# An attention sink folded into TensorE's accumulation, and the last score tile reduced in one piece

## The reference

```python
q = einsum('bsd,pd->bsp', x, w_q) + b_q          # 129 wide
k = einsum('bsd,pd->bsp', x, w_k) + b_k
v = einsum('bsd,ed->bse', x, w_v) + b_v
k_full = concatenate([k_0, k]);  v_full = concatenate([v_0, v])
attn = softmax(einsum('bqp,bkp->bqk', q, k_full))
x = layernorm(x + (x + einsum('bqk,bkd->bqd', attn, v_full)))
lilora_weight = up_aux @ (lora_up @ (lora_down @ down_aux))
x = layernorm(x + x @ W.T + b + x @ lilora_weight.T)
```

## Time and profile before

| | |
|---|---|
| time, median of 2 runs | 457.05 us (456.87 to 457.23) |
| the profiled execution's own time | 455.76 us |
| its span, slowest core (7) | 454.1 us |
| spans of the eight cores | 442.2 to 454.1 us |
| mean granted TensorE clock | 0.927 to 0.965 |
| busy: TensorE / VectorE / ScalarE | 370.0 / 227.8 / 105.7 us |

### The profile page before, as it was taken

The page is one execution under the profiler, slowest core; times in us unless marked ns, Lnnn a source line. Parts: engine busy times, 40 slices in busy tenths (PEclk is TensorE's granted clock), DMA queues, the critical chain, the costliest instruction groups (busy, mean ns, idle before and its releaser), DMA issues.

```text
span 454.1 us, 5184 instructions; the slowest of 8 cores (442.2 to 454.1 us)
## 1 busy us (share of the span) xinstructions
PE 370.0 (81%) x1861; PEld 156.0 (34%) x1861; DVE 227.8 (50%) x375; ACT 105.7 (23%) x119; POOL 22.5 (5%) x46
## 2 busy tenths in 40 slices
PE   0745999999878678889999999999745888899991
PEld 0211333333423223334444444444312334333330
DVE  7000033333399910004766677666688525677673
ACT  0203100000000048952121211212142232423332
POOL 8400000000000000010000000000110000000000
PEclk9997999999899969999999999999957559999997
DMA  8999300000000020024212213121390001232322
GB/s 126 166 168 168 52 0 0 1 0 0 1 1 1 0 93 0 1 44 103 64 49 62 78 48 95 46 81 59 69 149 16 0 1 46 95 139 104 130 122 110
DMA packets 11097, 28.25 MB, mean 62 GB/s; under 512 B 1856, under 2 KB 3008, under 8 KB 11072
## 3 DMA queue, kind: packets, MB, share of 16 engines
q0 software_dynamic: 5712, 10.52, 15.0%
q1 hardware_dynamic: 5360, 17.41, 11.0%
HBM read 29.50 MB, written 8.39 MB: 83 GB/s over the span
## 4 chain that ended last, share of the span: by engine, by line
issue 25%; DVE 24%; PEld 13%; PEldq 9%; DVEq 9%; DMA 8%; ACT 7%; POOL 3%; ACTq 0%; SPq 0%; POOLq 0%
DMA Ke<-PTsink 8%; PEld pv L377 5%; DVE pq L636 4%; PEld pq L516 4%; ACT o1s L746 4%; DVE mcols L588 4%; DVE X1f L665 3%; DVE st L654 2%; DVE ys L649 2%; PEldq L525 2%; DVEq L653 2%; DVEq L656 2%; PEldq L441 2%; DVE modd L592 2%; DVE modd L593 1%
## 5 line engine op out<-in xcount | busy, mean ns | idle before, releaser
L461 PE MATMUL pq<-Vh,AR 128*128 128x512 bf16 x256 | 97.2, 380 | 0.0
L460 PE MATMUL pq<-Vh,AR 128*128 128x512 bf16 x256 | 96.4, 377 | 0.0
L516 PE MATMUL pq<-Vh,AR 128*128 128x512 bf16 x256 | 62.3, 387 | 6.2 <-issue 5.0
L581 DVE TENSOR_TENSOR Vh<-pv,X1f 128x1024 bf16<-128x1024 f32 x16 | 19.6, 1226 | 84.9 <-PEq L381 84.9
L377 PE MATMUL pv<-AR 128*128 128x512 bf16 x256 | 57.8, 379 | 4.3 <-issue 3.5
L459 PE MATMUL pv<-Vh,AR 128*128 128x1 bf16 x256 | 42.0, 164 | 6.5 <-issue 4.8
L636 DVE SCALAR_TENSOR_TENSOR pq<-Vs,packf,pq 128x1024 f32<-128x1024 bf16 x16 | 20.6, 1289 | 48.0 <-PEq L462 45.5
L459 PEld LDWEIGHTS pv<-Vh,AR 128*128 128x128 bf16 x256 | 25.0, 98 | 42.7 <-issue 13.9
L516 PEld LDWEIGHTS pq<-Vh,AR 128*128 128x128 bf16 x256 | 24.2, 99 | 40.9 <-issue 15.8
L377 PEld LDWEIGHTS pv<-AR 128*128 128x128 bf16 x256 | 23.9, 97 | 38.2 <-issue 11.7
L460 PEld LDWEIGHTS pq<-Vh,AR 128*128 128x128 bf16 x256 | 24.5, 96 | 29.0
(11 more groups left out here) (134 smaller groups left out, 443.9 us busy)
## 6 DMA issues: line engine op xcount, KB each, us to landing
xs<-x SPq DMA_DIRECT2D x16, 512.0 KB, 3.7
out<-o1s SPq DMA_DIRECT2D x15, 512.0 KB, 2.8
AR<-xT POOLq DMA_DIRECT2D x7, 512.0 KB, 20.3
AR<-wvT POOLq DMA_DIRECT2D x8, 256.0 KB, 30.5
Vh<-WT POOLq DMA_DIRECT2D x8, 256.0 KB, 6.8
AR<-wqkT POOLq DMA_DIRECT2D x8, 64.5 KB, 15.3
X1f<-bvb SPq DMA_DIRECT2D x1, 512.0 KB, 3.3
AR<-xT POOLq DMA_DIRECT2D x2, 256.0 KB, 8.9
```

The lines of the kernel that those rows point to most:

```text
L460: te.matmul(PO[j % 2][:, 0:512], lhs, r1_, start=first, stop=last)
L461: te.matmul(PO[j % 2][:, 512:1024], lhs, r2_, start=first, stop=last)
L516: te.matmul(FO[j % 2][:, n0:n1], X1T[:, c * S + j * 128: c * S + (j + 1) * 128], WeffT[:, c * D + n0: c * D + n1], start=(c == 0), stop=False)
L581: ve.tensor_tensor(Vh[:, tt * VW: tt * VW + D], pv[tt % 2][:, :], bvbs[:, :], OP.add).then_inc(v, 1)
```

## The change

It has four parts.

1. **The sink goes through TensorE.** In pass C each tile has a 17th step of three matmuls, with `PTsink` (the sink's weights in row 0, zeros below) against `Vs` (the sink's value in row 0 and a one in the last column). `p6a_head` loses lines 636 and 639 and a drain.
2. **The sink's weights take the way of the maxima.** The transpose takes all 32 columns of `packf`, so it waits for `SC_PSINK` in place of `V_PACK`; a second DMA lays the 16 new rows out as row 0 of `PTsink`; pass B's waits ask for both DMAs on the count `dsy`, and the semaphore `dlp` goes.
3. **The last tile of pass A is reduced whole.** The mark `T_SA15H` goes, and the small operations run once, 16 wide, in place of 14 and then 2 wide.
4. **v_0 is loaded as one row** of 1024 in place of 128 equal rows.

```diff
-                g.dma_start(Vs[:, 0:D], v0r_d[:, :]).then_inc(dg, 16)
+                g.dma_start(Vs[0:1, 0:D], v0r_d[:, :]).then_inc(dg, 16)
...
                 sy.wait_ge(v, V_PACKT)
-                sy.dma_start(Qe2[1:2, :], packTf[0:16, :]).then_inc(dlp, 16)
+                sy.dma_start(Qe2[1:2, :], packTf[0:16, :]).then_inc(dsy, 16)
+                sy.dma_start(PTsink[0:1, :], packTf[16:32, :]).then_inc(dsy, 16)
...
-                        if j == NT - 1 and n == 1:
-                            te.drain(fusable=True).then_inc(t, 1)
                     te.drain(fusable=True).then_inc(t, 1)
-                te.wait_ge(v, V_PACK)
+                te.wait_ge(sc, SC_PSINK)
                 te.wait_ge(dsy, DSY_PRO)
-                te.matmul(pv[0][0:16, 0:128], packf[:, 0:16], idf[:, :],
+                te.matmul(pv[0][0:32, 0:128], packf[:, :], idf[:, :],
                           is_transpose=True, start=True, stop=True)
...
-                te.wait_ge(dlp, DLP_PACKT)
+                te.wait_ge(dsy, DSY_PACKT)
...
-                    for c in range(NT):
-                        first, last = (c == 0), (c == NT - 1)
+                    for c in range(NT + 1):
+                        first, last = (c == 0), (c == NT)
+                        if c < NT:
...
+                        else:
+                            lhs = PTsink[:, j * 128:(j + 1) * 128]
+                            r1_ = Vs[:, 0:512]
+                            r2_ = Vs[:, 512:1024]
+                            r3_ = Vs[:, D:VW]
...
                 def p6a_head(j):
                     p = j % 2
                     ve.wait_ge(t, TC(j))
-                    if j == 0:
-                        ve.wait_ge(sc, SC_PSINK)
-                    ve.scalar_tensor_tensor(PO[p][:, :], Vs[:, 0:D],
-                                            packf[:, 16 + j:17 + j],
-                                            PO[p][:, :], OP.mult, OP.add)
-                    ve.tensor_tensor(PL[p][:, 0:1], PL[p][:, 0:1],
-                                     packf[:, 16 + j:17 + j], OP.add)
-                    ve.drain()
                     ve.reciprocal(rls[p], PL[p][:, 0:1])
```

More of the change, by code:

```diff
@@ L28 @@
 T_SA0 = 20
-T_SA15H = 36
-T_SAF = lambda j: T_SA0 + j + 1 if j < NT - 1 else 37
-T_PACKT = 38
+T_PACKT = 37
 V_ONES = 1
@@ L157 @@
 SCD_OUT = lambda j: _SCD_OUT[j]
-DLP_PACKT = 16
+DSY_PACKT = DSY_PRO + 32
 DGP_ALL = 64
@@ L452, in _ @@
                         te.wait_ge(v, VC_RL(j - 2))
-                    for c in range(NT):
-                        first, last = (c == 0), (c == NT - 1)
[L455 to L458, removed]
+                    for c in range(NT + 1):
+                        first, last = (c == 0), (c == NT)
+                        if c < NT:
+                            lhs = PT[:, c * S + j * 128: c * S + (j + 1) * 128]
+                            r1_ = Vh[:, c * VW: c * VW + 512]
+                            r2_ = Vh[:, c * VW + 512: c * VW + 1024]
+                            r3_ = Vh[:, c * VW + D: c * VW + VW]
+                        else:
[3 more added lines that the diff above has]
+                            r3_ = Vs[:, D:VW]
                         te.matmul(PL[j % 2][:, 0:1], lhs, r3_, start=first, stop=last)
@@ L615, in _ @@
                 ve.drain()
-                ve.tensor_tensor(mcols[:, 15:16], modd[:, 14:15], modd[:, 15:16],
-                                 OP.max)
+                ve.tensor_tensor(bass.AP(mcols, 1, [[NT, 128], [2, 8]]),
+                                 bass.AP(modd, 0, [[NT, 128], [2, 8]]),
+                                 bass.AP(modd, 1, [[NT, 128], [2, 8]]), OP.max)
                 ve.drain()
-                ve.tensor_tensor(mcols[:, 14:16], mcols[:, 14:16],
-                                 ssink[:, 14:16], OP.max)
+                ve.tensor_tensor(mcols[:, :], mcols[:, :], ssink[:, :], OP.max)
@@ L621, in _ @@
                 ve.drain()
-                ve.tensor_scalar_mul(negmb[:, 14:16], mcols[:, 14:16], -1.0)
+                ve.tensor_scalar_mul(negmb[:, :], mcols[:, :], -1.0)
                 ve.drain()
-                ve.tensor_tensor(psd[:, 14:16], ssink[:, 14:16],
-                                 negmb[:, 14:16], OP.add)
-                ve.tensor_copy(packf[:, 14:16], negmb[:, 14:16])
+                ve.tensor_tensor(psd[:, :], ssink[:, :], negmb[:, :], OP.add)
+                ve.tensor_copy(packf[:, 0:16], negmb[:, :])
@@ L627, in _ @@
                 ve.drain().then_inc(v, 1)
                 ve.wait_ge(t, T_PACKT)
[L629 removed]
+                ve.tensor_copy(packTf[:, :], pv[0][0:32, 0:128]).then_inc(v, 1)
                 def p6a_head(j):
@@ L827 @@
         k0e=np.ascontiguousarray(k0[128:129, None]),
-        v0r=np.ascontiguousarray(np.tile(v0[None, :], (128, 1))),
+        v0r=np.ascontiguousarray(v0[None, :]),
         WT=np.ascontiguousarray(W.T),
```

28 lines of the change are left out of this document (3 added, 25 removed).

## The result

The changed kernel takes 455.13 us (median of 36 runs, 449.81 to 457.96), the kernel before 456.98 us (35 runs, 455.6 to 459.0): a ratio of 0.9949, interval 0.9936 to 0.9962. It is 0.5% faster, where 0.2% slower was forecast. The spread of its runs is more than twice as wide as before.

The account below looks back on a forecast made before the run. VectorE's chain, 8.01 us a tile against TensorE's 7.89, was taken to bound pass C and the merge. The terms -0.1 + 0.6 + 0.9 - 0.4 = +1.0 us gave 458.0 us; likeliest 456.5 to 459, range 454.0 to 460.5.

Parts of the forecast that it names:

- v_0 as one row: Wait before the first value matmul: the smaller load gives -0.1 us, ends 0 and -0.55.
- Last tile reduced whole: End of pass A: VectorE's maxima are ready 0.9 us earlier, ends 0.7 and 1.1.
- The wait for the sink's weight: Pack's transpose before pass B: waits for ScalarE's table load and exp, +1.48 us, +0.6 less the reductions' 0.9.
- The second DMA: Into pass B: lands under eight half-clock matmuls with 0.8 us to spare, costs nothing; ends 0 and +1.
- The 17th step: Pass C: TensorE pays 7.36 us, VectorE's relief returns 6.4, last reciprocal +0.9 us; ends +0.6 to +1.2.
- The merge: After pass C: TensorE's idle shrinks, so `B` runs at full clock, -0.4 us; ends -0.4 and 0.
- Rival A: Clock stays up through the merge: 446.1 us on all cores (0.05), or slowest a middling one, 450 to 454 (0.10).
- Rival B: Merge hangs on TensorE's end through W's DMA, not on VectorE's: 464.9 us, +1.7%; chance 0.06.
- Rival C: Second DMA or transposed pack shows: pass B's first sink matmul waits 1 to 2 us, 459 to 460; chance 0.09.

Follow-up runs that it names:

- E8: Changed kernel with useless matmuls in TensorE's merge waits, v_0 loaded as 128 rows again: 446.96 us, against 447.63 with one row.
- E4: Kernel before with useless matmuls in TensorE's merge waits and, of the change, only pass A's last tile reduced whole: 443.92 us.
- E5: E2 with the exp table loaded ahead, by a one-column exp before ScalarE's wait for the maxima: 444.77 us.
- E7: E2 with VectorE's two sink operations put back beside the 17th step, v_0 as 128 rows: 450.20 us.
- E6: E5 with only the last four tiles' sink through TensorE, the others' on VectorE, v_0 as 128 rows: 439.82 us.
- E3: Kernel before with 26 useless matmuls ahead of the merge's third transpose alone: 455.85 us, ratio 0.9973 to the kernel before.
- E2: Changed kernel with useless matmuls in TensorE's merge waits (2 ahead of B, 2 ahead of the first ct, 14 ahead of the third): 447.63 us.
- E10: E6 without the useless matmuls in the merge's waits: 450.18 us.

## Why the prediction was wrong

The time lies in the range, 455.1 in 454.0 to 460.5, but the kernel became 0.5% faster where 0.2% slower was forecast.

- **v_0 as one row, -0.1**: too small, with the ends 0 and -0.55. The average core starts its values 0.7 us sooner (E8 and the twelve profiled executions); on the slowest core nothing can be told. Of the 0.7 us, 0.4 lie in the wait before the first value matmul (0.85 us as a mean with one row, 1.25 with 128), which the sum read on two cores of one execution.
- **Last tile reduced whole, 0.9 us**: right, 1.0 in place (E4).
- **The wait for the sink's weight, +0.6 with the reductions**: right; 160.41 - 155.09 = 5.32 against 4.75, +0.57. Its size, 1.28 us for the table load without a drain, was confirmed by E5. Pass B as a whole took the same time in both kernels, 38.6 us as a mean of eight cores; that a shorter wait takes 0.7 to 0.8 us of half clock out of it (E4, E5) wasn't foreseen.
- **The second DMA, 0**: not tested by itself. The sink matmuls follow the eight at 164.37, and the DMA issued at 161.91 lands 1.7 us later by its row, at 163.6.
- **The 17th step, 7.36 paid and 6.4 got back, +0.9**: right in kind, +0.6 measured. A step costs 8.32 - 7.87 = 0.45 us. That it was VectorE's lag of 5.0 us, not its relief tile by tile, that gave the time back was shown by E7 and E6: with TensorE at 17 steps fifteen sinks are hidden, and four steps are enough.
- **The merge, -0.4**: `B` at 0.59 us, the third `ct` 0.3 us nearer to the reciprocal. That behind it VectorE's list sets the next start, whatever the clock is, holds for the third `ct`.
- **What failed** is the step after that one. The sum was made on core 7 and took everything behind the third `ct` as unchanged, a term of nothing; it measured -1.5 us between the slowest cores and -3.3 as the mean of the eight, 0.37 us for each microsecond less at half clock. Rival A, which names this mechanism, got 0.15, 0.10 of it for "the slowest is a middling one". The argument against A, that the wait before the third `ct` stays and grows, held on the cores that still had the full clock there: it grew to 3.8 and 3.9 us, they lost the clock in it, and they were the slowest two. But the argument took the clock as one state for all of the merge and for all cores. A core loses it for a time that differs from core to core: before, 44 us at 0.50 from 330 us on was the common case (cores 0, 3, 4 and 6 of the profile), after, it was 17 to 31 us. Five cores of the profile of before end at 453 to 454 us, all eight of the one after at 444 to 452, and over all runs the slowest fell by 2.3 us, over a path to the third `ct` that was 0.8 us longer. E3 shows the same in kind, and some three quarters of it, from the kernel before by covering its first idle stretch, without touching the path.
- Rival B is out: the first `ct` started 6.2 us after the last reciprocal, 6.6 before, although W's DMAs were issued 0.4 us after that reciprocal in place of 6.1 us ahead of it. Rival C didn't show.

That the time still lies in the range is no merit of the sum, which pointed the other way; it lies in the lower end, which rival A had opened.

What stays open: why a given core loses the full clock when it does, and gets it back when it does. The runs show where it is lost, in or right behind the waits of 2.9 us and more and, on most cores of the changed kernel, behind a row of gaps of 0.2 to 0.6 us; that 14 fillers bring it back and 18 to 42 mostly keep it; not what decides on a core whether it comes back after 17 or after 44 us.

## What to carry to other kernels

Before an operation is moved off an engine, find how far that engine lags at the end of the stage, and move only as many as the lag holds: four tiles of sixteen took up all of it here. Where a stage of short matmuls waits for another engine, look at the granted clock of every core, not of the slowest; a few useless matmuls in the waits gave 1.6% (the changed kernel to E2) to 2.3% (E10 to E6), more than the best of the path's changes without them (1.1%, the changed kernel to E10), and they have to fit into the wait at half clock too or they become the bound. With eight cores and a time set by the slowest, a change that moves the clock of most cores shows at a part of its worth, here somewhat over half, and its sign says little about the path: compare with the clock held up in both.

## What the runs showed of the hardware

TensorE was busy in 21.2 of 26 us and stayed at 1.2 GHz throughout (346 to 372 us on core 4 of the changed kernel), in short groups of matmuls and transposes with gaps of 0.34 us between them; on core 1 of the kernel before the same kinds of instructions ran at 2.4 GHz throughout. There TensorE was busy in 20.2 of 26 us, so how busy it looks doesn't tell the level. The Trainium skill, TensorE: Matmul & The Clock Gate, section What's actually happening, has it that activity releases the throttle; the trace agrees in so far as the clock came back in the end, while the engine worked, on every core (at 343 to 375 us before, at 352 to 373 after), though on core 4 of the changed kernel only after 27 us of such work.
